# A patch-embedding, gated-delta-rule and merged-FFN tower on one core: the norm factor and the decay column go through device memory, and block copies of the inverse go to GpSimd

## The reference

```
h   = embed(x)                                   # 48 pixels -> 128, bias, class token in front
xn  = layernorm(h)
q,k,v = causal 4-tap convolutions of linear maps of xn;  q,k = l2norm(silu(.)),  v = silu(.)
alpha, beta = sigmoid(linear(xn))                # one number for each token
S   = alpha * (S - beta * (S k) k^T) + beta * v k^T;   o = S q      # gated delta rule, token by token
h   = h + Wo(rmsnorm_zero_centred(o) * silu(Wg xn))
h2  = layernorm(h)
g   = mean over tokens of gate(h2)               # 8 mixing weights for each image
out = h + layernorm(h2 + relu(h2 W1m + b1m) W2m + b2m) * lng + lnb   # W1m, W2m mixed from 8 task vectors by g
```

## Time and profile before

| | us |
|---|---|
| median of 3 runs | 960.32 (959.33 to 962.34) |
| profiled execution, its own time | 962.57 |
| its span, first to last instruction | 960.6 |
| attention loop, from the first `xs` to the last gate | about 25 to 756 |
| FFN part | about 756 to 960 |

### The profile page before, as it was taken

One profiled execution on the slowest core, in us unless ns is written; L12 is line 12 of the kernel. 1 busy time (PEld: TensorE's weight loads), 2 busy tenths in 40 slices (PEclk: granted clock), 3 DMA queues, 4 the chain that ended last, 5 costly groups with the idle time before them and its releaser, 6 DMA issues. The chain is left out here.

```text
span 960.6 us, 31398 instructions
## 1 busy us (share of the span) xinstructions
PE 867.8 (90%) x11981; PEld 658.2 (69%) x11981; DVE 671.6 (70%) x2431; ACT 513.6 (53%) x1840; POOL 325.0 (34%) x430
## 2 busy tenths in 40 slices
PE   4699999999999999999999999999976789999995
PEld 2467767777777767777777777777764567677774
DVE  4366778777778777777787777777773566877433
ACT  0445456566655565656555656665534136665654
POOL 3112222222222222222222122222111148888875
PEclk9989899999999999999999999999997589999998
DMA  2000111111111000000000000000001214343331
GB/s 53 6 7 7 46 44 50 39 51 42 33 50 41 29 29 18 29 27 26 29 18 29 23 24 29 26 28 25 14 25 33 66 48 129 100 126 106 112 120 38
DMA packets 60185, 42.51 MB, mean 44 GB/s; under 512 B 3259, under 2 KB 52605, under 8 KB 60038
## 3 DMA queue, kind: packets, MB, share of 16 engines
q1 hardware_dynamic: 59189, 39.98, 13.8%
q10 hardware_dynamic: 848, 0.54, 0.2%
HBM read 20.97 MB, written 19.53 MB: 42 GB/s over the span
## 5 line engine op out<-in xcount | busy, mean ns | idle before, releaser
L1430 ACT ACTIVATE work<-bank,b1mix 128x512 f32<-128x512 f32 x96 | 66.0, 687 | 76.0 <-PE bank L1506 76.0
L1518 PEld LDWEIGHTS bank<-work 128*128 128x128 f32 x800 | 95.9, 197 | 15.1 <-issue 11.0
L408 ACT ACTIVATE logit<-bank 128x2 f32<-128x2 f32 x100 | 17.4, 174 | 163.6 <-PE bank L1010 163.6
L1518 PE MATMUL bank<-work 128*128 128x128 f32 x800 | 96.3, 280 | 3.2 <-DVE work L1348 3.2
L1009 PE MATMUL bank<-SA,work 128*128 128x386 f32 x200 | 94.8, 557 | 4.1 <-ACT work L511 2.9
L1506 PE MATMUL bank<-work 128*128 128x512 f32 x192 | 89.0, 607 | 0.9 <-DVE work L1348 0.9
L592 POOL TENSOR_TENSOR expo<-euler,logit 128x8 f32<-128x8 f32 x25 | 40.9, 1638 | 133.2 <-ACT logit L408 133.2
L1388 DVE TENSOR_TENSOR work<-bank,work 128x512 f32<-128x512 f32 x25 | 17.3, 692 | 64.8 <-PE bank L1518 64.8
L1010 PE MATMUL bank<-SB,work 128*128 128x256 f32 x200 | 61.3, 389 | 0.0
L1506 PEld LDWEIGHTS bank<-work 128*128 128x128 f32 x192 | 35.6, 196 | 37.2 <-issue 37.2
L612 POOL TENSOR_TENSOR oscale<-ovar,half_neg 128x4 f32<-128x4 f32 x25 | 25.2, 1007 | 103.9 <-DVE ovar L854 103.9
(11 more groups left out here) (222 smaller groups left out, 2323.3 us busy)
## 6 DMA issues: line engine op xcount, KB each, us to landing
hn_kept<-work SPq DMA_DIRECT2D x25, 256.0 KB, 2.3
hnT_kept<-work SPq DMA_DIRECT2D x25, 256.0 KB, 2.3
work<-hnT_kept SPq DMA_DIRECT2D x25, 256.0 KB, 2.9
work<-hn_kept SPq DMA_DIRECT2D x25, 256.0 KB, 3.1
out_dram<-work SPq DMA_DIRECT2D x24, 256.0 KB, 2.5
tv<-in_L_ffn_tv_W_dram SPq DMA_DIRECT2D x16, 256.0 KB
work<-in_x_dram SPq DMA_DIRECT2D x23, 102.0 KB
work<-in_projections_dram ACTq DMA_DIRECT2D x1, 257.0 KB
```

The costliest lines, as they stand in the source:

```text
L1430: ins = nc.scalar.activation(hid[f][:, :], ps[:, :], ACT.Relu, bias=b1mix[:, of[0], f:f + 1])
L1518: ins = mm(by4(bank[2 + par])[:, t, :], hid[f][:, t * C:(t + 1) * C], w2T[of[t]][:, f, :], start=(f == 0 and t == 0), stop=(f == FB - 1), ...
```

## The change

`rstd1` no longer goes through `rmat` and TensorE. SyncE stores it to device memory (512 elements of 4 bytes, transposed by the access pattern), waits for that store, and loads it back as rows, once broadcast over 49 partitions and once into one partition, into the new tile `rrows`. `decay` and the two rows of last values (now in one tile `decay_g`) go the same way: one store of a row, a wait, and two loads into `g_raw`, one as a column (512 elements of 4 bytes) and one broadcast over 128 partitions. The four `rmat` copies and transposes, the four one-row transposes, the matmul by ones and VectorE's copy L744 are gone. The six block copies L470 and L472 move from ScalarE to GpSimd. Level 6 of the inverse writes to bank 7 and its first product waits for `Y` alone, not for `X`. The transposes of `og` also write to bank 7, and `Wo` moves behind `km` of the next iteration. On VectorE the statistics of the first norm move ahead by one level, `kd`, `vmean` and `vt` move back, and the multiplication into `xs` moves from the end of the iteration to just ahead of level 5. On ScalarE the shifted copy moves ahead of the level 5 copies and the gate activations go behind `X6` and `ogT`.

```diff
+        r_dram = nc.dram_tensor("r_kept", (STEPS, NB, C), F32).ap()
+        g_dram = nc.dram_tensor("g_kept", (STEPS, NB * C + 2 * NB), F32).ap()
...
-        rmat = tile(NB * KX, NB, KX)
+        rrows = tile(NB * C, NB, C)
... SyncE, in body(j)
                     sp.dma_start(hn_dram[:, :, bass.ds(s, 1), :].rearrange("b p s c -> p b (s c)"), hn).then_inc(hn_out, 16)
+                if on(j, LE):
+                    s = j + LE
+                    sp.wait_ge(rstd1_ready, s + 1)
+                    sp.dma_start(r_dram[s].rearrange("b t -> t b"), rstd1[:, :], allow_slow_non_contiguous=True).then_inc(r_out, 16)
+                    sp.wait_ge(r_out, 16 * (s + 1))
+                    if s == 0:
+                        sp.wait_ge(rrows_set, 1)
+                    need(sp, xs_ready, s)
+                    sp.dma_start(rrows[0:PIX + 1], r_dram[s].partition_broadcast(PIX + 1)).then_inc(rrows_in, 16)
+                    sp.dma_start(rrows[PIX + 2:KX], r_dram[s:s + 1]).then_inc(rrows_in, 16)
+                if on(j, LH):
+                    s = j + LH
                     sp.wait_ge(hnT_ready, s + 1)
                     sp.dma_start(hnT_dram[:, :, bass.ds(s, 1), :].rearrange("b p s c -> p b (s c)"), hnT).then_inc(hnT_out, 16)
+                if on(j, LF):
+                    s = j + LF
+                    sp.wait_ge(glast_ready, s + 1)
+                    sp.dma_start(g_dram[s:s + 1, :], decay_g[0:1, :]).then_inc(g_out, 16)
+                    sp.wait_ge(g_out, 16 * (s + 1))
+                    need(sp, gs_ready, s - 1)
+                    need(sp, state_ready, s - 1)
+                    sp.dma_start(g_raw[s % 2][:, 0:NB], g_dram[s, 0:NB * C].rearrange("(b t) -> t b", b=NB), allow_slow_non_contiguous=True).then_inc(g_in[s % 2], 16)
+                    sp.dma_start(g_raw[s % 2][:, NB:3 * NB], g_dram[s, NB * C:NB * C + 2 * NB].partition_broadcast(D)).then_inc(g_in[s % 2], 16)
... ScalarE: behind the copy of hnT now stands the shifted copy of xs (was last)
-                    act.wait_ge(Y_ready, 5 * (s + 1))
-                    for r in (0, 1):
-                        nc.scalar.copy(Y[sub(r), :, sub(r)], Yd[par][sub(r)])
-                    for r in (2, 3, 0, 1):
-                        nc.scalar.copy(X[par][sub(r), :, sub(r)], Xd[par][sub(r)])
... and the gate activations (relu_h) stand last
... GpSimd: hist, rstd2, then var1e and rstd1, then expo, then the block copies, then oscale, knorm
-                    nc.gpsimd.tensor_copy(rmat[:, :, 0:PIX + 1], rstd1[:, :].unsqueeze(2).broadcast_to([D, NB, PIX + 1])).then_inc(rmat_ready, 1)
-                    nc.gpsimd.tensor_copy(rmat[:, :, PIX + 2:KX], rstd1[:, :].unsqueeze(2)).then_inc(rmat_ready, 1)
+                if on(j, LI):
+                    s = j + LI
+                    pool.wait_ge(Y_ready, 5 * (s + 1))
+                    for r in (0, 1):
+                        ins = nc.gpsimd.tensor_copy(Y[sub(r), :, sub(r)], Yd[par][sub(r)])
+                    ins.then_inc(Yd_kept, 1)
+                    for r in (2, 3, 0, 1):
+                        ins = nc.gpsimd.tensor_copy(X[par][sub(r), :, sub(r)], Xd[par][sub(r)])
+                    ins.then_inc(Xd_kept, 1)
+                    pool.wait_ge(Xd_kept, s + 1)
... VectorE
-                    nc.vector.tensor_copy(gs[par][:, 4:12], small_ps[:, 20:28]).then_inc(alpha0_kept, 1)
-                    nc.vector.tensor_tensor(gs[par][:, 0:4], small_ps[:, 16:20], gs[par][:, 8:12], ALU.mult).then_inc(gs_ready, 1)
+                    dve.wait_ge(g_in[par], 32 * (s // 2 + 1))
+                    nc.vector.tensor_tensor(gs[par][:, :], g_raw[par][:, 0:NB], g_raw[par][:, 2 * NB:3 * NB], ALU.mult).then_inc(gs_ready, 1)
... behind grow(2): the statistics of the first norm (were behind grow(3)); behind grow(3): expo1, ab, ab0, then kd;
... new_blocks(4); then vmean and vt; grow(4); o; and then
+                if on(j, LE):
+                    s = j + LE
+                    dve.wait_ge(rrows_in, 32 * (s + 1))
+                    dve.wait_ge(xt_in[par], 16 * (s // 2 + 1))
+                    nc.vector.tensor_tensor(xs[par][0:KX, :, HIST:XW], rrows[0:KX], xt[par][0:KX, :, :],
+                                            ALU.mult).then_inc(xs_ready, 1)
                 new_blocks(5)
... TensorE
-                        pe.wait_ge(X5_ready, s0 + 1)
+                        pe.wait_ge(Yd_kept, s0 + 1)
+                        pe.wait_ge(Y5_ready, s0 + 1)
+                        if C_:
+                            need(pe, ogT_ready, c)
...
+                if H_:
+                    pe.wait_ge(ogT_ready, h + 1)
+                    need(pe, hnT_ready, h)
+                    need(pe, o_ready, h + 1)
+                    for b in range(NB):
+                        ins = mm(by4(bank[6])[:, b, :], ogT[:, b, :], Wo_T[:, :], start=True, stop=True)
+                    ins.then_inc(wo_ps, 1)
                 level_blocks(1)
...
-                    for b in range(NB):
-                        ins = tr(by4(bank[1])[0:KX, b, :], rmat[:, b, :], ident[:, :])
-                    ins.then_inc(rb_ps, 1)
...
-                    for b in range(NB):
-                        tr(small_ps[:, 16 + b:17 + b], decay[0:1, b, :], ident[0:1, 0:1])
-                    mm(small_ps[:, 20:28], ones[0:1, :], glast[:, :], start=True, stop=True).then_inc(g_ps, 1)
```

More of the change, by code:

```diff
@@ L126, in vit_tower @@
         qT = [tile(NB * D, NB, D) for _ in range(2)]
-        decay = tile(NB * C, NB, C)
+        decay_g = tile(NB * C + 2 * NB)
+        decay = decay_g[:, 0:NB * C].rearrange("p (b c) -> p b c", b=NB)
+        glast = decay_g[0:1, NB * C:NB * C + 2 * NB]
         cdecay = tile(NB * C, NB, C)
@@ L175, in vit_tower @@
         qn2e = [sb(f"qn2e{i}", [D, NB]) for i in range(2)]
-        glast = sb("glast", [1, 2 * NB])
-        gs = [sb(f"gs{i}", [D, 12]) for i in range(2)]
+        gs = [sb(f"gs{i}", [D, NB]) for i in range(2)]
+        g_raw = [sb(f"g_raw{i}", [D, 3 * NB]) for i in range(2)]
         so2 = sb("so2", [D, NB])
@@ L487, in body @@
                     ins.then_inc(cdecay_ready, 1)
+                if on(j, LI):
+                    s = j + LI
+                    act.wait_ge(Xps_done, 6 * s + 6)
+                    nc.scalar.copy(X[par][0:64, :, 64:128], by64(X_ps)[0:64]).then_inc(X6_ready, 1)
+                if on(j, LC):
+                    s = j + LC
+                    act.wait_ge(ogT_ps, s + 1)
+                    need(act, wo_ps, s)
+                    nc.scalar.copy(ogT, by4(bank[7])).then_inc(ogT_ready, 1)
                 if on(j, LH):
@@ L828, in body @@
                     nc.vector.tensor_tensor(ab0[:, :], ab[:, 0:NB], not_first[:, :], ALU.mult).then_inc(ab0_ready, 1)
+                if on(j, LI):
+                    s = j + LI
+                    dve.wait_ge(cdecay_ready, s + 1)
+                    need(dve, dm_ps, s - 1)
+                    for b in range(NB):
+                        ins = nc.vector.tensor_scalar(kd[par][:, b, :], kvg[s % 3][:, b, 0:D], cdecay[:, b, C - 1:C], None, ALU.mult)
+                    ins.then_inc(kd_ready, 1)
+                new_blocks(4)
+                if on(j, LI):
+                    s = j + LI
+                    dve.wait_ge(vsum_ready, s + 1)
+                    need(dve, vt_ready, s)
+                    nc.vector.tensor_scalar(vmean[:, :], vsum[:, :], 1.0 / D, None, ALU.mult).then_inc(vmean_ready, 1)
+                    dve.wait_ge(knorm_ready, s + 1)
+                    dve.wait_ge(vmean_ready, s + 1)
+                    need(dve, Rn_ready, s - 1)
+                    for b in range(NB):
+                        ins = nc.vector.tensor_scalar(vt[par][:, b, :], kvg[s % 3][:, b, D:2 * D], vmean[:, b:b + 1], knorm[:, b:b + 1],
+                                                      ALU.subtract, ALU.mult)
+                    ins.then_inc(vt_ready, 1)
                 grow(4)
@@ L836, in body @@
                     nc.vector.tensor_tensor(o, by4(bank[6]), QMs, ALU.add).then_inc(o_ready, 1)
+                if isinstance(j, int) and j == first:
+                    fold_weights()
+                    sub_masks()
+                if on(j, LE):
+                    s = j + LE
+                    dve.wait_ge(rrows_in, 32 * (s + 1))
+                    dve.wait_ge(xt_in[par], 16 * (s // 2 + 1))
+                    need(dve, q_ps, s - 1)
+                    need(dve, hist_ready, s)
+                    nc.vector.tensor_tensor(xs[par][0:KX, :, HIST:XW], rrows[0:KX], xt[par][0:KX, :, :],
+                                            ALU.mult).then_inc(xs_ready, 1)
                 new_blocks(5)
@@ L975, in level_blocks @@
                         else:
-                            ins = mm(by64(blk_ps)[64:128, b], Bm[par][0:64, b, 64:128], Y[0:64, b, :], start=True, stop=True)
+                            ins = mm(by64(bank[7])[64:128, b], Bm[par][0:64, b, 64:128], Y[0:64, b, :], start=True, stop=True)
                     ins.then_inc(blk_ps_done, 1)
@@ L1013, in body @@
```

(1 more changed line is left out.)

153 lines of the change are left out of this document (48 added, 105 removed).

## The result

The changed kernel takes 1175.64 us (median of 4 runs, 1163.74 to 1180.30) where the kernel before takes 961.07 us (median of 4 runs, 959.33 to 962.34): a ratio of 1.2212, 95% interval 1.2133 to 1.2291. It is slower by 22%, against a forecast of 903 and a range that ended at 942.

A forecast was written before the change was run, and what follows sets the result against it. TensorE bounds the loop, busy 25.9 of 27.53 us; each period gains 1.66 + 1.06 less 0.2, 2.52 net. Times 23 is 58.0, less 1.5 at the start, plus 1.0 in the drain: 57.5, forecast 903 us, range 890 to 942.

The forecast's parts named there:

- the landing of the factor's store: SyncE's store of the norm factor, issued at 413.7, would land at 416.2, with 415.6 and 417.9 as bounds.
- What leaves TensorE: Between L1119 and L1147 on TensorE, a hole of 0.56, eight transposes and the matmul by ones go: 1.66 us each period.
- the hole ahead of L976: TensorE's wait ahead of level 6, ended by ScalarE's L477, would vanish: 1.06 us each period.
- GpSimd's copies: Six block copies on GpSimd at 0.28 us each, 1.7 in all (1.4 to 2.1), would cost nothing.
- VectorE ahead of level 5: VectorE's reordered work between levels 4 and 5 would add 0.2 us of stall each period, ends 0 and 0.6.
- The decay's way: Decay's store and loads through device memory would land before VectorE's L746 wants them: cost 0, at the upper end 1.2 us.
- The factor's way: Norm factor through device memory would land at 418.9 (418.3 to 422.5), wanted at 419.1: stall 0, upper end 3.3 us.
- The factor comes late: Rival, chance 0.23: slowly acknowledged 4-byte writes make the norm factor 1 to 2 us late each period; 937 us.
- slower: Rival, chance 0.08: both legs of the norm factor's trip take 4.2 us, 3.3 late each period; 979 us.
- The hold-up between VectorE and GpSimd: Rival, chance 0.17: GpSimd's block copies and VectorE's multiplication into `xs` exclude each other, 0.3 us each period; 910 us.

The follow-up runs named there:

- a_far64: The changed kernel with the factor's store in 512 pieces of 4 bytes 64 bytes apart, rows loaded from the input (factor wrong): 891.74 us, one run.
- b_pool: The kernel before with only the six block copies moved from ScalarE to GpSimd: 932.14 us, ratio 0.9699.
- a_16b: The changed kernel with the factor stored as 128 pieces of 16 bytes, VectorE reading the rows with a step of four: 901.43 us, ratio 0.9392 to the kernel before.

## Why the prediction was wrong

It is wrong in its sign and by 273 us. The step that failed is the landing of the factor's store: 2.5 us in the sum, 10.6 on average in the trace. With the loads behind it the wait decides the period, and the clock falls behind it.

- *What leaves TensorE, and the hole ahead of L976:* right. With a store that costs little the period is 24.70 or 24.67 us (forecast 25.0), which is 27.53 - 1.66 - 1.06 = 24.81 and a little more; TensorE is busy 467.10 of 468.55 us (a_far64). b_pool gives the second term alone, 1.11 for 1.06.
- *GpSimd's copies:* 0.286 us each (median of L630) and 1.88 for all six, where I took 1.7 with 1.4 to 2.1 as bounds; hidden, as said. Beside VectorE's multiplication they take 0.61 + 1.63 = 2.24 in a_far64, past the bound and still hidden; the last point has the reason.
- *VectorE ahead of level 5:* the order came as worked out, with the wait for `expo` (0.86 us); the 0.2 us of stall that I charged did not come in a_far64. In a_16b it came, and more, but for another reason: reading the rows with a step of four takes L870 from 0.68 to 1.06 us, the period to 25.18. The 901 us of a_16b so meet the forecast of 903 by the mechanism that it described, and in part by luck: a stall that was charged and did not come makes room for a slower multiplication that was not foreseen.
- *The decay's way:* right. Its store takes 1.74 us, its loads 2.1 and 2.7 to landing, and no wait of VectorE for them is among those of the changed kernel.
- *The factor's way, the step that failed.* I took 2.5 us for the store (413.7 to 416.2), with 1.9 and 4.2 as ends; it took 9.63 in the period shown, 10.59 on average, and 9.4 in iteration -1, where no store of `hn` is ahead of it. The upper end was the slowest transfer of a period, and I said myself that no transfer of 4-byte elements stood there. The bound was none: with the pieces spread or joined the same 2 KB need 2.5 us from issue to loads (a_far64, a_16b), as I took; side by side they need four times that. The loads took 4.3 us in the period shown and 3.74 on average, where I took 2.7 from the first issue; in a_16b the step takes 2.9, so that size was right without the crowded store.
- *The rivals.* "The factor comes late" and "slower" had the right mechanism, VectorE idle ahead of the multiplication and TensorE ahead of level 5, with 0.31 of the chance between them. Only "slower", with 0.08, had the right sign; the late factor's 937 us are still faster than before. Their price was wrong twice. The multiplication was wanted 419.2 - 413.3 = 5.9 us behind the store of `hn` and starts 14.75 behind it on average, so the lateness is 8.9 us and not 1.5 or 3.3. And they carried the lateness over to the time one to one. TensorE is indeed idle for 8.6 us of each period, but behind that hole its clock falls, and the same work takes 28.17 us instead of 24.58, 3.6 more. I looked for a loss of clock in a denser loop, and it came in a thinner one.
- *The hold-up between VectorE and GpSimd:* it is there, but it falls on the other engine. In the changed kernel the factor comes so late that the multiplication and the copies do not meet. In a_far64 they do:

```profile
436.27 0.71 DVE L870 TENSOR_TENSOR work<-work 51x512 f32<-51x512 f32 x1
```

```profile
436.50 1.63 POOL L630 COPY work<-work 32x128 f32<-32x128 f32 x4
```

The four copies take 1.63 us instead of the 1.27 of the changed kernel, and the longest single one 0.704 instead of 0.293. In a_16b, where the multiplication is longer, that is 2.04 in one period and 1.19 for the longest. The trace so agrees with the rule of the Trainium skill that the prediction names (SBUF: State Buffer, Who interferes with whom). VectorE loses only 0.03 us (0.71 against 0.68) where I priced 0.3, and GpSimd's loss is hidden.

The rule of the Trainium skill that I weighed (DMA: Bandwidth & Descriptors, Rules for kernel authors: a strided last dimension becomes one descriptor for each element, rearrange) pointed at the right instruction. The runs do not agree with it as an account of the cost: 512 separate elements 64 bytes apart are as quick as 128 pieces of 16 bytes (a wait of 1.7 us in both). The 2.0 us of fixed cost that the prediction took from the Trainium skill (DMA: Bandwidth & Descriptors, Anatomy of one DMA) stand in a section on transfers issued from GpSimd, while SyncE issues these. Taken as an estimate for them, they fit the spread store (1.7 us) and fail for the crowded one (9.8).

## What to carry to other kernels

Before a small transposed store goes on a path, look at what it writes and not at how much: let few pieces fall close together in device memory (here up to 4 in each 64 bytes did no harm, and 8 did), by keeping each partition's elements together and putting the order right at the reader. A kind of transfer that the trace does not hold has no upper bound there; then the range must include the case in which the new wait decides, and a wait of some microseconds on TensorE must be priced with the slower clock behind it. A DMA that nobody waits for is not thereby free, and a short stop can cost more through the clock behind it than by itself.

## What the runs showed of the hardware that I had not expected

- A store of 2 KB in 512 pieces of 4 bytes side by side keeps SyncE waiting for 9.8 us on average; the same pieces 8 bytes apart 3.4 to 3.6, 64 bytes apart 1.7. Loads in pieces of 4 bytes do not have this: the decay's column landed 2.1 us after issue.
- While such a store is pending, VectorE stands still in some iterations, until 8.7 to 9.0 us after its issue in the three looked at, also in a kernel where nothing on the way waits for it (980.75 us against 958.55). Most of that loss is the lower clock: in the long period shown 3.0 of 3.5 us.
- In a hole of 3.9 us on TensorE the granted clock fell to 0.50 at about 440, and with a second hole behind it stayed there until about 457, though TensorE was busy without a break from 447.5 on.
- A VectorE multiplication with both inputs in the state buffer and GpSimd's copies there exclude each other: the four copies took 1.63 us beside it and 1.27 alone.
- VectorE's multiplication of 51x512 took 1.06 us with one input read in steps of four elements, and 0.68 without.
